# A new slot plan for the attention pipeline: probability transposes in three groups a pair, five probability buffers

## The reference

```python
c_q = hidden @ w_q_down                       # 512 -> 192
q_nope, q_rope = c_q @ w_q_up_nope, c_q @ w_q_up_rope   # 32 heads, 128 and 64 wide
c_kv, k_rope = hidden @ w_kv_down, hidden @ w_k_rope     # 64 and 64 wide, shared by all heads
q_rope, k_rope = rope(q_rope), rope(k_rope)
q_lat = einsum('bhsd,hdr->bhsr', q_nope, wuk)            # 64 wide
scores = (q_lat @ c_kv.T + q_rope @ k_rope.T) / sqrt(192)
probs = softmax(where(causal, scores, min))
out_lat = probs @ c_kv                                   # 64 wide
out = (out_lat with w_uv, then w_out)                    # 512 wide, added to x
```

## Time and profile before

| | us |
|---|---|
| median of 3 runs | 1338.89 (1338.37 to 1340.07) |
| the profiled execution | 1338.54 |
| its span, first to last instruction | 1336.6 |
| TensorE busy, weight loads busy | 1200.8, 1013.3 |
| VectorE, ScalarE, GpSimd busy | 849.3, 638.9, 513.5 |
| mean granted TensorE clock, share of full | 0.968 |

### The profile page before, as it was taken

How to read it: one execution, slowest core, us unless ns; L and a number is a source line. 1 busy time by engine, 2 the same in 40 slices (tenths; PEclk the granted TensorE clock), 3 DMA queues, 4 the chain that set the end, 5 groups by cost and what they waited for, 6 DMA issues and landing times.

```text
span 1336.6 us, 27786 instructions
## 1 busy us (share of the span) xinstructions
PE 1200.8 (90%) x8424; PEld 1013.3 (76%) x8424; DVE 849.3 (64%) x3266; ACT 638.9 (48%) x1810; POOL 513.5 (38%) x821
## 2 busy tenths in 40 slices
PE   3587899999988799999989699999989789999996
PEld 3465788888777688888768678888869678888876
DVE  1564666667667566676667466676666666666755
ACT  1433555555413455555513365555532365555641
POOL 0311544444312454444422254444430254544430
PEclk8798999999989899999989899999998899999998
DMA  9251000000000000000010000000010000000000
GB/s 270 84 154 59 1 1 1 0 0 2 33 24 10 3 2 1 0 0 1 2 32 33 3 1 1 0 0 1 1 33 33 1 1 1 1 0 0 2 1 32
DMA packets 21232, 27.64 MB, mean 21 GB/s; under 512 B 9942, under 2 KB 11734, under 8 KB 20474
## 3 DMA queue, kind: packets, MB, share of 16 engines
q1 hardware_dynamic: 16922, 17.98, 4.2%
q10 hardware_dynamic: 4192, 8.19, 2.1%
HBM read 21.97 MB, written 4.19 MB: 20 GB/s over the span
## 4 chain that ended last, share of the span: by engine, by line
PE 67%; issue 15%; DVE 10%; ACT 3%; POOL 2%; DVEq 0%; POOLq 0%; ACTq 0%
PE Y L932 12%; PE Y L906 10%; PE XZ L891 9%; PE Y L840 8%; PE XZ L870 5%; PE Y L747 5%; PE XZ L872 4%; PE XZ L871 4%; PE XZ L747 3%; PE Y L852 3%; PE XZ L720 1%; PE Y L793 1%; DVE small L1342 1%; DVE qT_lo L1290 1%; DVE XZ L1342 1%
## 5 line engine op out<-in xcount | busy, mean ns | idle before, releaser
L701 POOL TENSOR_TENSOR prob<-prob,small 128x512 f32<-128x512 f32 (+3 forms) x512 | 361.3, 722 | 433.9 <-DVE small L1297 432.9
L1342 DVE CUSTOM_DVE_ANT_0 XZ<-XZ,mask 128x512 f32<-128x512 f32 (+3 forms) x512 | 244.3, 508 | 286.4 <-issue 283.3
L1078 ACT ACTIVATE prob<-XZ,small 128x512 f32<-128x512 f32 (+3 forms) x512 | 267.1, 526 | 288.4 <-DVE small L1342 288.3
L870 PE MATMUL XZ<-kT_hi,qT_hi 128*128 128x512 f32 (+3 forms) x512 | 186.9, 365 | 25.4 <-DVE qT_lo L1290 14.9
L891 PE MATMUL XZ<-ident,prob 128*128 128x128 f32 x1280 | 195.6, 275 | 0.2
L872 PE MATMUL XZ<-kT_hi,qT_lo 128*128 128x512 f32 (+3 forms) x512 | 166.8, 326 | 0.0
L871 PE MATMUL XZ<-kT_lo,qT_hi 128*128 128x512 f32 (+3 forms) x512 | 166.2, 325 | 0.0
L891 PEld LDWEIGHTS XZ<-ident,prob 128*128 128x128 f32 x1280 | 147.6, 140 | 21.1 <-POOL prob L701 7.3
L906 PE MATMUL Y<-probT,ckv 128*64 128x384 f32 (+2 forms) x1280 | 152.3, 384 | 8.7 <-ACT probT L596 8.0
L596 ACT ACTIVATE probT<-XZ 128x512 f32<-128x512 f32 x192 | 114.8, 598 | 79.5 <-PE XZ L891 77.2
L906 PEld LDWEIGHTS Y<-probT,ckv 128*64 128x64 f32 x1280 | 84.0, 136 | 71.5 <-issue 44.9
(11 more groups left out here) (203 smaller groups left out, 2512.5 us busy)
## 6 DMA issues: line engine op xcount, KB each, us to landing
wout_nat<-in_L_attn_w_out_dram SPq DMA_DIRECT2D x8, 1024.0 KB, 5.9
out_dram<-x_sb SPq DMA_DIRECT2D x16, 256.0 KB, 2.0
x_next<-_attn_hidden_states_dram SPq DMA_DIRECT2D x12, 256.0 KB, 3.1
nope_a<-_L_attn_w_q_up_nope_dram ACTq DMA_DIRECT2D x2, 1024.0 KB, 14.1
wbase_nat<-in_L_ffn_W_base_dram ACTq DMA_DIRECT2D x1, 1024.0 KB, 5.5
nope_b<-_L_attn_w_q_up_nope_dram ACTq DMA_DIRECT2D x2, 512.0 KB, 13.1
rope_a<-_L_attn_w_q_up_rope_dram ACTq DMA_DIRECT2D x1, 1024.0 KB, 10.7
rope_bb<-_L_attn_w_q_up_rope_dram ACTq DMA_DIRECT2D x2, 512.0 KB, 13.1
```

Of the source, the lines that this page charges most:

```text
L701: last = nc.gpsimd.tensor_tensor(prob[u % RING][:, c:c + w], prob[u % RING][:, c:c + w], inv_sum[:, u % RING, m:m + 1].broadcast_to([P, w] ...
L870: nc.tensor.matmul(bank[:, c:c + w], high, kT_hi[:, 0:w], start=True, stop=False)
L1078: last = nc.scalar.activation(prob[u % RING][:, c:c + w], score_ps[u % 2][:, c:c + w], ACT.Exp, bias=neg_max[:, u % RING, m:m + 1], scale= ...
L1342: last = nc.vector.tensor_tensor_reduce(bank, bank, mask[:, S - w:S], -1.0, HIGHEST, ALU.add, ALU.min, neg_max[:, u % RING, m:m + 1])
```

## The change

- Two tables `T_LAGS` and `ready_units` take the place of the fixed lag of 3: probability transposes are made only in slots with k = 0 (unit 2 of the pair before), k = 2 (units 3 and 4 of the pair before) and k = 4 (units 0 and 1 of this pair, behind the latent product). The copies to `probT` follow them.
- The latent product moves from k = 3 to k = 4, and within a slot the order on TensorE becomes: scores, query products, output, latent product, probability transposes, query transposes.
- The output product at k = 4 moves to k = 3; in the tail the last two go to its first two slots.
- The query transposes move from k = 1 and 3 to k = 2 and 3, both at the end of the slot; `qT_high` and `qT_low` move from k = 2 and 4 to k = 3 and 4. `q_products`, `q_rotary` and ScalarE's `q_latent` stay where they are.
- `RING` goes from 4 to 5, so there is one more probability buffer of 2 KB a partition and the columns of `small` move; `dynamic_dma_scratch_size` goes from 4096 to 2048.

```diff
-RING = 4
-T_LAG = 3
-PV_SLOT = 3
+RING = 5
+T_LAGS = {0: (3,), 2: (4, 3), 4: (4, 3)}
+PV_SLOT, PV_SLOT_TAIL = 4, 3
-OUT_SLOT = {1: 0, 4: 1}
-OUT_SLOT_TAIL = {1: 0, 2: 1}
+OUT_SLOT = {1: 0, 3: 1}
+OUT_SLOT_TAIL = {0: 0, 1: 1}
...
-        small = place("small", [P, 60], F32)
+        small = place("small", [P, 67], F32)
...
+        def ready_units(g, u):
+            return [u - lag for lag in T_LAGS.get(u % UNITS, ())
+                    if known(g, u, lag) and within(g, u - lag, SLOTS - 1)]
...
                         if k in (0, 2) and queries:
                             q_products(b, n, k // 2, False)
-                        if k == PV_SLOT and known(g, u, UNITS):
-                            pv(b, g, p - 1)
-                        if known(g, u, T_LAG) and within(g, u, SLOTS - 1 + T_LAG):
-                            transpose_probs(b, g, u - T_LAG)
                         if output_rows(u) is not None and known(g, u, 3 * UNITS):
                             output(b, g, p, output_rows(u))
-                        if k in (1, 3) and queries:
-                            q_transposes(b, n, k // 2, False)
+                        if k == (PV_SLOT if u < BODY else PV_SLOT_TAIL) and known(g, u, UNITS):
+                            pv(b, g, p - 1)
+                        for v in ready_units(g, u):
+                            transpose_probs(b, g, v)
+                        if k in (2, 3) and queries:
+                            q_transposes(b, n, k - 2, False)
...
-                        if k in (2, 4) and queries:
-                            qT_high(b, n1, k // 2 - 1, (p + 1) % 2)
+                        if k in (3, 4) and queries:
+                            qT_high(b, n1, k - 3, (p + 1) % 2)
...
-                        if k in (2, 4) and queries:
-                            qT_low(b, n1, k // 2 - 1, (p + 1) % 2)
+                        if k in (3, 4) and queries:
+                            qT_low(b, n1, k - 3, (p + 1) % 2)
...
-    nc = _bacc.Bacc("TRN2", target_bir_lowering=False, num_devices=1, dynamic_dma_scratch_size=4096)
+    nc = _bacc.Bacc("TRN2", target_bir_lowering=False, num_devices=1, dynamic_dma_scratch_size=2048)
```

More of the change, by code:

```diff
@@ L151, in build @@
         neg_max = columns(28, 2 * RING).rearrange("p (r m) -> p r m", m=2)
[L152 to L155, removed]
+        row_sum = columns(38, 2 * RING).rearrange("p (r m) -> p r m", m=2)
+        inv_sum = columns(48, 2 * RING).rearrange("p (r m) -> p r m", m=2)
+        ones, eps, minus_half = columns(58, 2), columns(60, 1), columns(61, 1)
+        wait_slots = small[0:1, 62:67]
         region_a = [cursor[0]]
@@ L568, in output_rows @@
             slots = OUT_SLOT if u < BODY else OUT_SLOT_TAIL
-            return 2 * ((p + 1) % 2) + slots[k] if k in slots else None
+            return 2 * ((p + 1) % 2) + slots[k] if k in slots and u < BODY + UNITS else None
+        def ready_units(g, u):
+            return [u - lag for lag in T_LAGS.get(u % UNITS, ())
+                    if known(g, u, lag) and within(g, u - lag, SLOTS - 1)]
         def oT_buffer(q):
@@ L1081, in work @@
                             last.then_inc(prob_set, 1)
-                        v = u - T_LAG
-                        if known(g, u, T_LAG) and within(g, u, SLOTS - 1 + T_LAG) and v % UNITS in ACT_BANKS:
-                            copy_probT(act, nc.scalar, b, g, v)
+                        for v in ready_units(g, u):
+                            if v % UNITS in ACT_BANKS:
+                                copy_probT(act, nc.scalar, b, g, v)
                     attention((b, act), work, TAIL)
@@ L1356, in work @@
                             row_moments(DOWN - 1).then_inc(var_set, 1)
-                        v = u - T_LAG
-                        if known(g, u, T_LAG) and within(g, u, SLOTS - 1 + T_LAG) and v % UNITS not in ACT_BANKS:
-                            copy_probT(dve, nc.vector, b, g, v)
+                        for v in ready_units(g, u):
+                            if v % UNITS not in ACT_BANKS:
+                                copy_probT(dve, nc.vector, b, g, v)
                         if output_rows(u) is not None and known(g, u, 3 * UNITS):
```

## The result

| | before | after |
|---|---|---|
| median, us | 1339.16 (4 runs, 1338.37 to 1340.07) | 1394.45 (4 runs, 1392.41 to 1399.38) |
| the profiled execution, us | 1338.54 | 1394.20 |
| TensorE busy, us | 1200.8 | 1201.4 |
| a full pair, us | 14.73 | 15.58 |
| from the first scores of attention to the first transposes behind it, four batch entries, us | 249.3, 249.0, 250.4, 247.2 | 262.4, 260.2, 263.6, 261.1 |

The changed kernel takes 1.0418 times as long (95% interval 1.039 to 1.0446). The forecast was slower, and slower it is, but by 55.7 us (profiled executions) and not by 8.6; the time lies above the stated range, which ended at 1362.

What follows compares the result with a forecast made beforehand. TensorE was taken to bound attention. Full pairs at -0.54 + 0.94 = +0.40 make +19.2 over 48; with -3.4, -0.9 and -6.3 that is +8.6, so 1347 us; forecast case's range 1341 to 1357, whole range 1334 to 1362.

Steps and rivals of the forecast that it cites:

- the new wait: Query half 1's transposes on TensorE wait for VectorE's split of query half 0: 0.94 us a pair added.
- the last bodies: Last written-out body of each batch entry: no term for a VectorE pause there, put at nothing.
- The start: First transfers and the beginning of attention: no term, put at nothing.
- The chain: From half 0's first transpose through VectorE's rotation, copy, minima and split to TensorE: 3.57 us, 3.74 at the upper end.
- The cover: TensorE's work meanwhile, half 0's transposes, a unit of scores and an output product: 2.63 us.
- The gain behind transposes: Three fewer places a pair where a matmul follows transposes, each 0.09 us: 0.27 saved.
- the fitting rival: The 0.09 behind transposes comes back elsewhere, a full pair is +0.67, time 1361 us; chance 0.10.
- The sign named for it: In the profile after, output products would show 0.23 us at their first matmul; 0.32 would refute it.
- The waits removed: Waits at a new pair's scores (0.09 us) and at the latent product (0.18 us) go.
- Nothing for the rest: Fifth buffer, smaller scratch, moved columns and feed-forward steps were to cost nothing.
- The rival of the falling clock: TensorE's clock falls by 7% in the attention pairs: +51 us, so 1398; chance 0.04.
- The pairs that are not full: First pairs of bodies -3.4 us, early pairs 1 and 2 -0.9, last pairs -6.3; tail counted as even.

Runs made afterwards that it cites:

- e1: Changed kernel with VectorE's split of query half 0 directly behind the rotation of query half 1, ahead of unit 3's copy and minima: 1318.24 us, ratio 0.9847.
- e5: Changed kernel with only VectorE's copy of unit 3 moved behind the split of query half 0: 1362.35 us, ratio 1.0167.
- e2: Changed kernel with query half 0 back in its old places, transposed in slot 1 and split in slots 2 and 4: 1323.91 us, ratio 0.989.
- e7: Kernel before with only the small tile at 67 columns in place of 60: 1343.91 us, ratio 1.0025.
- e11: Kernel before with five probability buffers and the scratch of 2048, small tile at its old size: 1337.07 us, ratio 0.9987.
- e6: Kernel before with only the smaller scratch of 2048: 1340.11 us, ratio 0.9992.
- e9: e1 with the wait columns in unused ones, so the small tile keeps its old size: 1314.87 us, ratio 0.9818.
- e10: e9 with the loop's last output product moved from the tail's second slot to its fourth: 1311.13 us, ratio 0.9791.
- e3: Kernel before with the output product ahead of the latent product and probability transposes within a slot: 1356.41 us, ratio 1.0128.
- e4: Kernel before with only five probability buffers, the moved columns and the scratch of 2048: 1343.94 us, ratio 1.0038.
- e8: e1 with a small tile of 80 columns, so the tiles behind lie 64 bytes off in place of 32: 1319.86 us, ratio 0.9844.

## Why the prediction was wrong

The direction and the new wait were right. Two steps failed: a gain was counted that does not exist, 13 us (2), and the last bodies, put at nothing, lost 13.7 us (4). The start, also put at nothing, lost 3.9 (5). The rest are sizes.

1. **The new wait: right in kind and place, small in size.** Predicted 0.94, measured 1.06. The chain took 3.74 and not 3.57: 0.71 for the first piece (305.26 to 305.97) and not 0.64, and a handoff of 0.15 (308.85 to 309.00) and not 0.07. The cover was 2.68 and not 2.63. Over 48 pairs that is 6 us. e1 and e5 show that this wait is the loss: with it a pair takes 15.58, with 0.60 less 14.98, without it 14.52.

2. **The gain behind transposes: the step that failed.** "3 x 0.09 = 0.27" doesn't exist. The 0.09 at the next matmul is matched by 0.08 that the last transpose of the group is drawn short. I read one side of it, and gave the fitting rival one chance in ten. e2's pair of 14.50, where 14.3 was due by this step, shows it: 13 us of the miss. The sign named for it came true all the same: the output's first matmul takes 0.24 at one place (300.93 to 301.17) and 0.28 at the other (306.51 to 306.79). A sign read at one border can't tell the two readings apart.

   The Trainium skill (TensorE: Matmul & The Clock Gate, Part 2) says that the next tile's weights load while this tile's matmul runs. The prediction drew from it that the order costs nothing, and e2's 14.50 agrees; my row was no evidence against it.

3. **The waits removed: half right.** The one at the new pair's scores is gone (0.09). At the latent product 0.18 was counted, but with its copies long done it still starts 0.21 behind a score matmul of 256 columns (310.05 to 310.26), where another score matmul would follow in 0.12: 0.09 is the way in. So a full pair gained 0.21, and not 0.54: with the wait's 1.06 that is the +0.85.

4. **The last bodies: a term put at nothing, and the second step that failed.** The part headed "Nothing for the rest" had no term for them. VectorE's pause of 1.7 us was in the trace before, at 1.95 us of idle time, and was covered. The change took the cover away, and the pause then held TensorE: idle 2.62, 2.70, 2.69 and 2.91 where a usual pair has 0.90, which is 7.3 us in all. Behind three of these four the clock fell (0.57, 0.51 and 0.58 in the 4 us behind), and nearly all of the other 6.4 lies in those three entries; behind the 2.70 it stayed at 1.00. Together 13.7 us, a quarter of the loss. The rival of the falling clock, which would have it fall in every pair, was wrong: the waits of 1.06 do nothing to it (1.00 in the window from 250). In the pairs it fell only behind longer ones, those three and one of the early waits of 2.3, while the other waits of that size left it at 1.00. What the pause itself is (it stands in the last, written-out body of each entry, and is no wait that the profile names) stays open; that it is the fetch of instructions was not tested.

5. **The start: costed at nothing, 3.9 us.** That "the moved columns touch no transfer in attention" was true, but they moved the targets of the transfers at the start. e7 and e11 show that this lengthens the transfers (18.6 and 14.1) and the time (1.0025 and 0.9987 of the kernel before). That all of the 3.9 comes from it is not shown: e6, with its tiles on a multiple of 512, also began attention 2.9 later than the kernel before, in its one profile.

6. **The pairs that are not full.** Predicted -0.9 for the early pairs and -6.3 for the last ones, measured +2.9 and -2.8. The early wait was 2.48 and not 2.32, by the same longer chain as in step 1; the pair around it had less saved, by the steps 2 and 3, and one fall of the clock. In the tail the last latent product waits for ScalarE (0.69 in e9), which e10 removed.

Sum of the misses: 21.6 in the full pairs, 13.7, 3.9 and about 8: the 47 between 8.6 and 55.7.

## What to carry to other kernels

When a slot plan moves a producer later, write down for each single buffer (here one PSUM bank and one token tile) what lies on the helper engine's queue between the event that frees it and the instruction that frees it again: here one instruction's place in VectorE's list was worth 76 us of 1394. Take the cost of a kind of work between two far starts, never at one border: here the profile drew a border's cost on both sides of it. And an engine that comes onto the critical chain brings its rare pauses with it: look for them in its idle time before, at loop ends above all.

## What the runs showed of the hardware

- Transposes of 128x128 fp32 take 0.109 us each from start to start (eight with four more behind in 0.87). Where another kind follows, the group is drawn 0.08 short (eight in 0.79 and four in 0.36, e2) and the next matmul some 0.09 long.
- Idle times of 2.62, 2.69 and 2.91 us on TensorE left a granted clock of 0.57, 0.51 and 0.58 in the 4 us behind them, and one of 2.70 left it at 1.00. Waits of 1.06 in every pair left it at 1.00, and idle times of 2.3 mostly did, but once it was 0.60 behind one.
- Transfers of 1 MB into tiles that start on a multiple of 512 bytes landed in 13.9 to 14.9 us (before, e3, e6, e9 to e11); into tiles 32 or 64 bytes off in 16.7 to 18.6 (after, e1, e2, e4, e5, e7, e8). No other offset was tried. The kernel's time followed by 0.25 to 0.5% (e7 1.0025, e4 1.0038, e11 0.9987 of the kernel before).
